# w_down turned by transposing transfers and clipped in two places, the last pair's u by halves, new orders

## The chip, the cores and the metric

The kernel runs on one core of a Trainium2 chip. The metric is the device time of one execution in microseconds: the median of three runs, 260.02 us before the change (259.32 to 260.18). The engines are named as in the profile: PE is TensorE, PEld its weight loads, DVE is VectorE, ACT is ScalarE, POOL is GpSimd, SP is SyncE. A "q" behind a name is the queue from which that engine issues transfers.

## The reference, cut to what matters

```python
def fwht(x): ...             # normalised Walsh-Hadamard transform, last axis
def act_quant(x, bits):      # per token: round(x * 127 / max|x|), clipped, divided again
def weight_quant(w):
    scale = jnp.clip(jnp.mean(jnp.abs(w)), EPS, None)
    q = jnp.clip(jnp.round(w / scale), -1.0, 1.0) * scale
def hbitlinear(x, w, bits):
    xq = act_quant(fwht(x), bits)
    wq = weight_quant(w)
    return jnp.einsum('bsd,fd->bsf', xq, wq)

w = weights[conditions]                        # x: (64, 64, 512), w: (64, 64, 64)
h = jnp.einsum('bct,bcd->bdt', x, w)           # conditional projection
h = hbitlinear(h, w_up, 8)                     # 512 -> 1024
h = jnp.square(jax.nn.relu(h))
x = x + hbitlinear(h, w_down, 8)               # 1024 -> 512
```

## The kernel before

The 64 batches of 64 rows are 16 tiles of 256 tokens; a tile t has two halves k of 128 tokens (a "pair" of batches). For each tile TensorE runs `project(t)` (the conditional product with the first steps of the Hadamard transform, fp32, L870), `had_z(t,k)` (the 128-wide Hadamard step, fp32, L886), `up(t,u)` for u = 0 to 3 (fp16, L911), `had_u(t,k)` (the 128-wide Hadamard step of h, fp32, L934) and `down(t,k)` (fp16, L966). Between them ScalarE copies (`y_split`, L508), quantises z and u to fp16 (`quant_z` L519, `quant_u` L566), applies relu (L526) and square (L533), and issues the transposing transfers of the quantised tiles (`turn_z` L541, `turn_u` L559). VectorE runs the other Hadamard steps (`y_outer` L1207, `g_outer` L1240, `g_inner` L1245), the maxima (`z_absmax` L1224, `u_absmax` L1252) with a small `floor` and `invert` behind each, and the `residual` (L1270), which adds x and writes the output tile. GpSimd runs the last addition and subtraction of a half's Hadamard transform (`g_last`, L373, two instructions) and small factors (`token_units` L358, `u_unscale` L379). SyncE issues the loads of x (L201), the gathers of the conditional weights (L208) and the stores (L222).

Every engine's order is written out by hand as a list of calls, and every call waits on semaphores. u_ps holds one half of u only, so each `had_u` waits until `quant_u` has read the half before it; the second halves of the last two tiles have a home of their own in h_ps. A load of x(t) waits for the residuals of tile t - 8.

The weights: w_up and w_down each come as four pieces of 128 x 1024 fp32. Their absolute values are summed, one scale comes of that, and ScalarE multiplies each piece by the inverse scale into fp16 units of 2^-24 (`weight_round`, L493), where the conversion rounds. `weight_turn` (L854) turns a piece in eight 128x128 transposes on TensorE into u_ps, and `weight_evac` (L1201) copies it out on VectorE with both clips to w_upT or w_downT. `weight_turn(n, u)` for u of 2 or 3 waits for the evacuation two before it. `had_u(0,0)` waits for the evacuations of w_down, as they share u_ps; `down(0,0)` waits for w_downT.

The end: `had_u(15,1)`, `down(13,1)`, `had_u(15,0)`, `down(14,1)`, `down(14,0)`, then both quantised halves of the last tile are turned on TensorE (`last_turn`, L942) and copied by VectorE (`last_copy`, L1219), and `down(15,0)` and `down(15,1)` follow, each with its residual and store.

Of the kernel before, what the change touches and what calls it, by code (L numbers as in the profile page):

```python
# [13 lines left out]
P = 128  # L14
B, C, T = 64, 64, 512
F = 1024
KP = 2
# [27 lines left out]
def ffn_kernel(nc, x, cond, w_cond, w_up, w_down, had, out):  # L45
# [7 lines left out]
    with ctx:  # L53
# [20 lines left out]
        w_downT = sb("w_downT", [P, FC, T], FP16)  # L74
# [18 lines left out]
        u_max = sb("u_max", [P, TILES, KP], FP32)  # L93
        u_abs = sb("u_abs", [P, TILES, KP], FP32)
# [23 lines left out]

        s_cond = sem("cond_loaded")
# [15 lines left out]
        s_wT = [sems(f"wT_ready{n}", 4) for n in range(2)]  # L135
        s_turn = sem("turn_may_start")
# [31 lines left out]
        s_table = sem("table_loaded")  # L168
        s_o = sems("o_ready", KP)
# [27 lines left out]
        def _(sp):  # L197
# [20 lines left out]

            def store(t, k):
# [25 lines left out]
            gather(3, 0)  # L245
            gather(3, 1)
            load_x(3)
# [7 lines left out]
            gather(5, 1)  # L255
            load_x(4)
            load_x(5)
            gather(5, 2)
# [9 lines left out]
            gather(8, 0)  # L268
            gather(8, 1)
            gather(8, 2)  # L270
            load_x(6)
            gather(8, 3)
            load_x(7)
            gather(9, 0)
            gather(9, 1)
            gather(9, 2)
            store(0, 1)
            load_x(8)
            gather(9, 3)
# [3 lines left out]
            store(0, 0)  # L283
# [3 lines left out]
            store(1, 1)  # L287
            store(1, 0)
            load_x(9)
            store(2, 1)  # L290
            gather(11, 2)
            gather(11, 3)
            load_x(10)
            gather(12, 0)
            store(2, 0)
            load_x(11)
            gather(12, 1)
            gather(12, 2)
            gather(12, 3)
            store(3, 1)  # L300
            gather(13, 0)
            gather(13, 1)
            gather(13, 2)
            gather(13, 3)
            gather(14, 0)
            gather(14, 1)
            store(3, 0)
            store(4, 1)
            store(4, 0)
            gather(14, 2)  # L310
            load_x(12)
            gather(14, 3)
            store(5, 0)
            gather(15, 0)
            store(5, 1)
            load_x(13)
            gather(15, 1)
            load_x(14)
            gather(15, 2)
            store(6, 1)  # L320
            store(6, 0)
            load_x(15)
            store(7, 1)
            gather(15, 3)
            store(8, 1)
            store(7, 0)
            store(8, 0)
            store(9, 0)
            store(9, 1)
            store(10, 1)  # L330
            store(10, 0)
            store(11, 1)
            store(11, 0)
            store(12, 0)
            store(12, 1)
            store(13, 1)
            store(13, 0)
            store(14, 0)
            store(15, 0)
            store(14, 1)  # L340
            store(15, 1)
            for i in range(NO):
                for k in range(KP):
                    sp.wait_ge(s_store[i][k], 16 * (TILES // NO))

        @block.gpsimd
        def _(pool):
# [4 lines left out]
                                    base=0, pattern=[[-1, P]], channel_multiplier=1).then_inc(s_ident, 1)  # L352

# [1287 lines left out]
```

## Time and profile before

| | |
|---|---|
| median of three runs | 260.02 us (259.32 to 260.18) |
| the profiled execution | 260.16 us |
| its span, first to last instruction | 258.4 us |
| TensorE busy | 250.6 us, 97% |
| VectorE busy | 206.6 us, 80% |
| ScalarE busy | 146.9 us, 57% |
| GpSimd busy | 107.9 us, 42% |
| DMA, mean | 133 GB/s |

An engine's busy time counts the instructions that work on data; issuing a transfer and waiting don't count. The ends of matmuls are modelled, so the time from the start of a group of matmuls to the start of the next tells more than its busy time. In a timeline a row is a run of equal instructions: start, length, engine, line, operation, output and input, count, and in brackets how long the engine stood idle before it and what released it.

### The profile page before, as it was taken

How to read it: one execution, taken by the hardware profiler on the slowest of the kernel's cores; microseconds unless marked ns; L12 is line 12 of the kernel's file. 1: busy time of each engine (PE TensorE's matmuls, PEld its weight loads, DVE VectorE, ACT ScalarE, POOL GpSimd, SP SyncE). 2: the span in 40 equal slices, each digit the busy share in tenths (PEclk: the TensorE clock that was granted, in tenths of full speed). 3: DMA queues.
4: the chain of work that ended last, by engine and by line, in shares of the span. 5: the costliest groups of instructions: out<-in, count | busy, mean ns of one | idle time of the engine just before them, and what ended most of it. 6: DMA issues, size and time to landing. Idle time of an engine off the chain costs nothing. (4 is left out here: it accounts for less than half of the span.)

```text
span 258.4 us, 6363 instructions
## 1 busy us (share of the span) xinstructions
PE 250.6 (97%) x2218; PEld 208.8 (81%) x2218; DVE 206.6 (80%) x344; ACT 146.9 (57%) x210; POOL 107.9 (42%) x135
## 2 busy tenths in 40 slices
PE   8999999999999999999999999999999999989994
PEld 8988898989888788778997788878898887757651
DVE  0468599979998597897878987989898898999482
ACT  0279797577445756375657275555775647551330
POOL 1000008580707336260807353472935545686710
PEclk9999999999999999999999999999999999999999
DMA  4995162264383272846634981364446757435523
GB/s 109 356 373 186 40 193 54 55 189 91 65 205 97 43 209 57 173 107 156 105 89 124 205 210 26 74 195 83 127 80 86 201 115 133 124 92 109 126 109 137
DMA packets 63442, 34.31 MB, mean 133 GB/s; under 512 B 53554, under 2 KB 53682, under 8 KB 63410
## 3 DMA queue, kind: packets, MB, share of 16 engines
q10 hardware_dynamic: 48370, 12.95, 27.4%
q1 hardware_dynamic: 15040, 20.95, 25.2%
q8 instruction: 18, 0.29, 0.5%
q14 instruction: 14, 0.11, 0.1%
HBM read 13.70 MB, written 8.39 MB: 85 GB/s over the span
## 5 line engine op out<-in xcount | busy, mean ns | idle before, releaser
L373 POOL TENSOR_TENSOR p<-g 128x512 f32<-128x512 f32 x64 | 80.8, 1286 | 126.8 <-DVE g L1245 126.8
L911 PE MATMUL h_ps<-zqT,w_upT 128*128 128x256 f16 x512 | 63.5, 273 | 0.0
L934 PE MATMUL u_ps<-had_sb,p 128*128 128x128 f32 x480 | 59.0, 276 | 1.8 <-ACT uq L566 1.8
L934 PEld LDWEIGHTS u_ps<-had_sb,p 128*128 128x128 f32 x480 | 56.6, 192 | 4.7 <-ACT uq L566 3.2
L966 PE MATMUL o_ps<-w_downT,uqT 128*128 128x512 f16 x240 | 56.7, 379 | 0.2 <-DVE uqT L1219 0.2
L911 PEld LDWEIGHTS h_ps<-zqT,w_upT 128*128 128x128 f16 x512 | 49.4, 98 | 7.8
L566 ACT ACTIVATE uq<-u_ps,u_mul 128x1024 f16<-128x1024 f32 x30 | 33.4, 1112 | 33.9 <-DVE u_mul L1263 27.9
L526 ACT ACTIVATE g<-h_ps 128x512 f32<-128x512 f32 x64 | 37.3, 594 | 25.9 <-PE h_ps L911 18.9
L1252 DVE TENSOR_REDUCE u_max<-u_ps 128x1 f32<-128x1024 f32 x30 | 36.6, 1220 | 11.9 <-PE u_ps L934 11.6
L966 PEld LDWEIGHTS o_ps<-w_downT,uqT 128*128 128x128 f16 x240 | 23.4, 98 | 22.3 <-issue 0.4
L1240 DVE TENSOR_TENSOR g<-g 128x1024 f32<-128x1024 f32 x32 | 40.4, 1288 | 1.0 <-issue 0.7
L1245 DVE TENSOR_TENSOR g<-g 128x1024 f32<-128x1024 f32 x32 | 38.2, 1216 | 0.2
L533 ACT ACTIVATE g<-g 128x1024 f32<-128x1024 f32 x32 | 33.3, 1054 | 3.9 <-issue 2.8
L886 PE MATMUL z_ps<-had_sb,y 128*128 128x128 f32 x248 | 33.6, 278 | 0.3 <-ACT zq L519 0.2
L870 PE MATMUL y_ps<-ws,xs 64*128 64x128 f32 x512 | 32.9, 278 | 0.1
L870 PEld LDWEIGHTS y_ps<-ws,xs 64*128 64x128 f32 x512 | 29.9, 188 | 3.1 <-issue 2.1
L886 PEld LDWEIGHTS z_ps<-had_sb,y 128*128 128x128 f32 x248 | 30.5, 192 | 2.1 <-ACT zq L519 0.7
L519 ACT ACTIVATE zq<-z_ps,z_col 128x512 f16<-128x512 f32 x31 | 21.2, 683 | 17.2 <-DVE z_col L1234 16.1
L1270 DVE SCALAR_TENSOR_TENSOR out_sb<-o_ps,u_deq,xs 128x512 f32<-128x512 f32 x30 | 22.4, 747 | 9.3 <-PE o_ps L966 9.0
L1224 DVE TENSOR_REDUCE z_max<-z_ps 128x1 f32<-128x512 f32 x31 | 21.2, 685 | 6.9 <-PE z_ps L886 6.8
L1207 DVE TENSOR_TENSOR y<-y_ps,y_odd 128x512 f32<-128x512 f32 x32 | 21.1, 684 | 2.6 <-ACT y_odd L508 2.6
L379 POOL TENSOR_SCALAR u_deq<-kappa,down_scale,u_abs 128x1 f32<-128x1 f32 x32 | 17.7, 564 | 5.3 <-DVE u_abs L1258 5.2
(54 smaller groups left out, 136.5 us busy)
## 6 DMA issues: line engine op xcount, KB each, us to landing
xs<-in_x_dram SPq DMA_DIRECT2D x16, 512.0 KB, 4.2
out_dram<-out_sb SPq DMA_DIRECT2D x32, 256.0 KB, 2.4
w_raw<-in_L_ffn_w_down_dram SPq DMA_DIRECT2D x4, 512.0 KB, 6.7
w_raw<-in_L_ffn_w_up_dram ACTq DMA_DIRECT2D x2, 512.0 KB, 5.9
w_raw<-in_L_ffn_w_up_dram SPq DMA_DIRECT2D x2, 512.0 KB, 6.7
ws<-in_L_cond_weights_dram SPq DMA_DIRECT2D x62, 16.0 KB, 2.4
uqT<-uq ACTq DMA_TRANSPOSE x30, 3.2
zqT<-zq ACTq DMA_TRANSPOSE x15, 3.3
```

Of the source, the lines that this page charges most:

```text
L373: nc.gpsimd.tensor_tensor(new[:, :, m, :], old[:, :, 0, :], old[:, :, 1, :], (ALU.add, ALU.subtract)[m]).then_inc(s_p8[k], 1)
L526: nc.scalar.activation(g[t % 2][:, 2 * u:2 * u + 2, :], h_ps[:, u % 2, :, :], ACT.Relu, scale=1.0 / UNIT).then_inc(s_r[u], 1)
L533: nc.scalar.activation(part, part, ACT.Square).then_inc(s_g[v], 1)
L566: nc.scalar.activation(uq[t % 2][:, k, :], u_home(t, k), ACT.Copy, scale=u_mul[:, t, k:k + 1])\
L870: mm = nc.tensor.matmul(y_ps[:, b, l, :, j, :], xs[t % NX][rows, j, h * 256 + l * P:h * 256 + (l + 1) * P], w, start=(h == 0), stop=(h == 1))
L886: mm = nc.tensor.matmul(z_home(t, k)[:, c * P:(c + 1) * P], y[t % 2][:, c % 2, c // 2, k, :, :].rearrange("p b d -> p (b d)"), had_sb[:, : ...
L911: mm = nc.tensor.matmul(h_ps[:, u % 2, i, :].rearrange("p (k n) -> p k n", k=KP), w_upT[:, q, f * P:(f + 1) * P], zqT[t % NZT][:, :, q, :] ...
L934: mm = nc.tensor.matmul(home[:, c * P:(c + 1) * P], p8[t % 2][:, c, k * P:(k + 1) * P], had_sb[:, :], start=True, stop=True)
L966: mm = nc.tensor.matmul(o_home(t, k), uqT[t % 2][:, k, m, :], w_downT[:, m, :], start=(m == 0), stop=(m == FC - 1))
L1240: nc.vector.tensor_tensor(g2[:, n, :, :], g[t % 2][:, 0:4, :], g[t % 2][:, 4:8, :], (ALU.add, ALU.subtract)[n]).then_inc(s_g2, 1)
L1245: nc.vector.tensor_tensor(p4[t % 2][:, :, n, :], g2[:, :, 0:2, :].rearrange("p h a n -> p h (a n)"), g2[:, :, 2:4, :].rearrange("p h a n - ...
L1252: nc.vector.tensor_reduce(u_max[:, t, k:k + 1], u_home(t, k), AX.X, ALU.max, apply_absolute_value=True).then_inc(s_umax[k], 1)
```

## The change

w_down: `weight_round(1, u)` goes from ScalarE to GpSimd, with the clip from above in the same instruction. A new `weight_clip(u)` on VectorE clips from below, in place in SBUF. A new `turn_w(u)` on ScalarE issues a transposing transfer of the piece into w_downT, which is laid out anew ([P, 4, FC, P] instead of [P, FC, T]). The four `weight_turn(1, u)` on TensorE, the four `weight_evac(1, u)` on VectorE and the waits of `had_u(0,0)` go.

The last half, (15,1): `had_u` is cut into two halves of 512 columns, each with its own absmax; one quantisation goes to ScalarE and one to VectorE, the two turned halves go to two homes and are copied by VectorE and ScalarE, and `down` is cut into two halves of 256 output columns, each with its residual and its own store, one issued by SyncE and one by ScalarE.

The orders of all five engines are laid anew. The core:

```diff
-        w_downT = sb("w_downT", [P, FC, T], FP16)
+        w_downT = sb("w_downT", [P, 4, FC, P], FP16)
...
+        HF, HT = F // 2, T // 2
+        uT_half = [uT_ps[1][:, 0:HF], u_ps[:, 0:HT].bitcast(FP16)]
+        o_half = [z_ps[:, 0:HT], u_ps[:, T:T + HT]]
...
+            def weight_round(n, u):
+                pool.wait_ge(s_winv[n], 1)
+                nc.gpsimd.tensor_scalar(w_int[n][u], w_raw[n][:, u * WQ:(u + 1) * WQ], w_inv[:, n:n + 1], UNIT,
+                                        ALU.mult, ALU.min).then_inc(s_wrint[n][u], 1)
...
+            weight_round(1, 0)
+            weight_round(1, 1)
+            weight_round(1, 2)
             g_last(0, 0)
+            weight_round(1, 3)
             token_units(0)
...
+            def turn_w(u):
+                act.wait_ge(s_wclip[u], 1)
+                act.sem_inc(s_turn, 1)
+                act.dma_start(w_downT[:, u, :, :], w_int[1][u], transpose=True).then_inc(s_wT[1][u], 16)
...
+            def quant_half():
+                u_turned(act, TILES - 3, 1)
+                act.wait_ge(s_umul[1], TILES)
+                nc.scalar.activation(uq[(TILES - 1) % 2][:, 1, 0:HF], h_flat[:, 0:HF], ACT.Copy,
+                                     scale=u_mul[:, TILES - 1, 1:2]).then_inc(s_uqhalf[0], 1)
...
             quant_z(2, 0)
+            turn_w(0)
             y_split(3)
+            turn_w(1)
+            relu(1, 0)
             relu(1, 1)
...
+            turn_w(2)
             square(1, 0)
             quant_z(2, 1)
...
             quant_z(3, 0)
+            turn_w(3)
             quant_u(0, 0)
...
+            quant_half()
             quant_u(15, 0)
-            quant_u(15, 1)
+            copy_half_too(1)
+            store_half_too(1)
...
-                if t == 0 and k == 0:
-                    pe.wait_ge(s_wT[1][2], 1)
-                    pe.wait_ge(s_wT[1][3], 1)
...
+            def down_half(c):
+                if c == 0:
+                    pe.wait_ge(s_out[1], TILES - 1)
+                for h in range(2):
+                    pe.wait_ge(s_uqThalf[h], 1)
+                for m in range(FC):
+                    mm = nc.tensor.matmul(o_half[c].rearrange("p (u n) -> p u n", u=2), uqT[(TILES - 1) % 2][:, 1, m, :],
+                                          w_downT[:, 2 * c:2 * c + 2, m, :],
+                                          start=(m == 0), stop=(m == FC - 1))
+                mm.then_inc(s_ohalf[c], 1)
...
             down(13, 0)
-            had_u(15, 1)
+            had_half(0)
+            had_half(1)
             down(13, 1)
             had_u(15, 0)
             down(14, 1)
+            turn_half(0)
             down(14, 0)
+            turn_half(1)
             last_turn(0)
-            last_turn(1)
+            down_half(0)
             down(15, 0)
-            down(15, 1)
+            down_half(1)
...
+            def weight_clip(u):
+                dve.wait_ge(s_wrint[1][u], 1)
+                nc.vector.tensor_scalar(w_int[1][u], w_int[1][u], -UNIT, None, ALU.max)\
+                    .then_inc(s_wclip[u], 1)
```

TensorE's order of the head, before and after (from `had_z(1,1)` to `had_u(0,0)`):

```
before: had_z(1,1) project(2) up(0,2) up(0,3) weight_turn(1,0) had_z(2,0) project(3) up(1,0) up(1,1) had_z(2,1)
        weight_turn(1,2) up(1,3) weight_turn(1,1) project(4) weight_turn(1,3) up(1,2) had_z(3,0) had_u(0,0)
after:  had_z(1,1) project(2) up(0,3) up(0,2) had_z(2,0) project(3) had_z(2,1) up(1,0) up(1,1) up(1,2) up(1,3)
        project(4) had_z(3,0) had_u(0,0)
```

VectorE's order in the same stretch:

```
before: y_outer(2,0) y_outer(2,1) z_absmax(2,0) weight_evac(1,0) ... g_outer(0,0) g_outer(0,1) y_outer(3,0)
        y_outer(3,1) g_inner(0,0) g_inner(0,1) weight_evac(1,1) z_absmax(2,1) ...
after:  y_outer(2,1) y_outer(2,0) weight_clip(1) weight_clip(0) z_absmax(2,0) ... g_outer(0,0) g_outer(0,1)
        weight_clip(2) g_inner(0,1) g_inner(0,0) y_outer(3,1) y_outer(3,0) z_absmax(2,1) ...
```

TensorE's order ahead of the end:

```
before: had_u(12,1) down(10,1) up(15,0) up(15,1) down(11,0) had_u(13,0) up(15,2) up(15,3) down(11,1) had_u(13,1)
        down(12,0) had_u(14,1) down(12,1) had_u(14,0) down(13,0) had_u(15,1) ...
after:  down(10,1) up(14,3) up(14,2) had_u(12,1) down(11,0) up(15,0) up(15,1) had_u(13,0) up(15,3) up(15,2)
        down(11,1) down(12,0) had_u(13,1) had_u(14,1) down(12,1) had_u(14,0) down(13,0) had_half(0) had_half(1) ...
```

VectorE's order between `u_absmax(12,1)` and `g_inner(15,1)` is nearly the same in both; after: `g_outer(14)`, `g_inner(14)`, `u_absmax(13,0)`, `residual(11,1)`, `g_outer(15)`, `g_inner(15,0)`, `u_absmax(13,1)`, `residual(12,0)`, `u_absmax(14,1)`, `g_inner(15,1)`.

## Rows read from the trace of the kernel before

**Rows 1.** The page, part 1: busy us, share of the span, instructions.

```profile
PE 250.6 (97%) x2218; PEld 208.8 (81%) x2218; DVE 206.6 (80%) x344; ACT 146.9 (57%) x210; POOL 107.9 (42%) x135
```

**Rows 2.** Stretches: us, busy us of each engine, TensorE's clock, DMA share, GB/s.

```profile
27.00:44.00 17.00, 16.78 (x206) 15.26 (x203) 14.30 (x26) 13.63 (x21) 4.00 (x7) 1.00 0.34 96
...
55.00:215.00 160.00, 159.39 (x1412) 133.47 (x1410) 137.45 (x230) 96.36 (x140) 73.37 (x95) 1.00 0.56 126
215.00:240.00 25.00, 23.81 (x170) 17.70 (x168) 22.47 (x29) 11.65 (x14) 18.14 (x14) 1.00 0.48 114
```

**Rows 3.** TensorE's waits: waited for, us in total, times, longest.

```profile
PE u_ps L934 <- ACT uq L566: 1.8, 2, 1.2
```

**Rows 4.** Timeline of TensorE in the head.

```profile
36.62 0.61 PE L854 MATMUL u_ps<-ident,w_raw 128*128 128x128 f16 x8
37.06 1.04 PE L911 MATMUL h_ps<-zqT,w_upT 128*128 128x256 f16 x8
...
38.48 2.06 PE L870 MATMUL y_ps<-ws,xs 64*128 64x128 f32 x32
...
43.18 1.95 PE L934 MATMUL u_ps<-had_sb,p 128*128 128x128 f32 x16
```

**Rows 5.** Groups by line: shapes, count, busy us, mean ns, idle before.

```profile
L493 ACT ACTIVATE w_raw<-w_raw,w_inv 128x1024 f16<-128x1024 f32 x8 | 8.9, 1144 | 0.0
L1229 DVE TENSOR_SCALAR z_col<-z_max 128x1 f32<-128x1 f32 x32 | 4.8, 150 | 0.6
L1201 DVE TENSOR_SCALAR w_downT<-u_ps 128x1024 f16<-128x1024 f16 x4 | 2.6, 679 | 0.0
```

**Rows 6.** Timeline of ScalarE and of its queue (ACTq).

```profile
42.22 1.27 ACTq L541 DMA_TRANSPOSE zqT<-zq  x1
43.54 0.60 ACT L526 ACTIVATE g<-h_ps 128x512 f32<-128x512 f32 x1 [0.93 <-issue]
```

**Rows 7.** Timeline of VectorE in the head.

```profile
25.82 0.16 DVE L1181 RECIPROCAL w_inv<-w_scale 128x1 f32<-128x1 f32 x1
...
32.09 0.69 DVE L1224 TENSOR_REDUCE z_max<-z_ps 128x1 f32<-128x512 f32 x1 [1.31 <-PE z_ps L886]
33.94 2.36 DVE L1240 TENSOR_TENSOR g<-g 128x1024 f32<-128x1024 f32 x2 [0.30 <-ACT g L533]
36.22 1.28 DVE L1207 TENSOR_TENSOR y<-y_ps,y_odd 128x512 f32<-128x512 f32 x2
37.41 2.35 DVE L1245 TENSOR_TENSOR g<-g 128x1024 f32<-128x1024 f32 x2
```

**Rows 8.** Timeline of GpSimd in the head.

```profile
39.85 2.50 POOL L373 TENSOR_TENSOR p<-g 128x512 f32<-128x512 f32 x2 [38.23 <-DVE g L1245]
46.90 2.45 POOL L379 TENSOR_SCALAR u_deq<-kappa,down_scale,u_abs 128x1 f32<-128x1 f32 x1 [1.24 <-DVE u_abs L1258]
```

**Rows 9.** Timeline of TensorE near 110 us; then landings of x, 150 to 185 us.

```profile
110.17 1.05 PE L934 MATMUL u_ps<-had_sb,p 128*128 128x128 f32 x7 [0.61 <-ACT uq L566]
...
DMA to landing us min/median/max: 4.2/4.3/4.8
```

**Rows 10.** Timeline ahead of the end; then two pieces of the chain that ended last.

```profile
216.38 1.95 PE L934 MATMUL u_ps<-had_sb,p 128*128 128x128 f32 x16
...
236.72 1.22 DVE L1245 TENSOR_TENSOR g<-g 128x1024 f32<-128x1024 f32 x1
...
240.73 2.02 PE L934 MATMUL h_ps<-had_sb,p 128*128 128x128 f32 x16
...
237.27 1.78 PE u_ps L934 x16
239.06 1.73 PE o_ps L966 x8
```

**Rows 11.** Timeline of the end.

```profile
255.09 0.75 DVE L1270 SCALAR_TENSOR_TENSOR out_sb<-z_ps,u_deq,xs 128x512 f32<-128x512 f32 x1 [0.98 <-PE z_ps L966]
```

**Rows 12.** The page, part 6: issues, KB each, median us to landing.

```profile
out_dram<-out_sb SPq DMA_DIRECT2D x32, 256.0 KB, 2.4
```

More of the change, by code:

```diff
@@ L680, in _ @@
+            quant_z(8, 0)
+            turn_z(7)
             relu(6, 0)
-            quant_z(8, 0)
-            relu(6, 1)
-            turn_u(3, 1)
+            quant_u(4, 0)
             y_split(9)
-            relu(6, 2)
-            turn_z(7)
-            quant_u(4, 0)
+            negate_w(10)
+            quant_z(8, 1)
             relu(6, 3)
             square(6, 0)
+            quant_u(4, 1)
+            turn_z(8)
+            relu(6, 2)
             square(6, 1)
+            relu(7, 1)
@@ L721, in _ @@
+            quant_z(10, 0)
+            negate_w(12)
+            y_split(11)
+            turn_u(5, 1)
+            quant_u(6, 1)
+            square(8, 0)
+            quant_z(10, 1)
+            negate_w(13)
+            relu(8, 3)
             square(8, 1)
-            quant_u(6, 1)
+            turn_z(10)
+            relu(9, 1)
             relu(9, 0)
+            y_split(12)
+            quant_u(7, 0)
+            relu(9, 3)
+            quant_z(11, 0)
             turn_u(6, 1)
-            quant_z(10, 1)
@@ L1058, in _ @@
             down(3, 0)
+            project(9)
             had_u(4, 1)
+            up(6, 2)
             down(3, 1)
             up(7, 1)
+            had_u(5, 0)
             had_z(9, 0)
             up(7, 0)
-            had_u(5, 0)
             project(10)
             up(7, 2)
-            down(4, 0)
             up(7, 3)
@@ L1461, in _ @@
             y_outer(11, 0)
-            g_outer(8, 0)
             y_outer(11, 1)
+            z_absmax(10, 1)
+            z_floor(10, 1)
+            z_invert(10, 1)
             residual(5, 0)
             u_absmax(7, 0)
+            g_outer(8, 1)
+            g_outer(8, 0)
             u_floor(7, 0)
+            residual(5, 1)
+            z_absmax(11, 0)
+            g_inner(8, 1)
+            z_floor(11, 0)
             u_invert(7, 0)
-            z_absmax(11, 0)
-            g_outer(8, 1)
@@ L1470, in _ @@
[L1470 to L1472 removed]
             g_inner(8, 0)
+            y_outer(12, 0)
+            z_invert(11, 0)
+            residual(6, 0)
+            y_outer(12, 1)
             u_absmax(7, 1)
[L1475 to L1476 removed]
             u_floor(7, 1)
             u_invert(7, 1)
[L1479 removed]
             z_absmax(11, 1)
             z_floor(11, 1)
+            g_outer(9, 0)
             z_invert(11, 1)
+            g_outer(9, 1)
@@ L1528, in _ @@
             z_invert(13, 1)
+            g_outer(11, 1)
+            g_inner(11, 1)
             g_inner(11, 0)
-            g_inner(11, 1)
+            residual(8, 0)
             z_absmax(14, 0)
@@ L1539, in _ @@
             residual(8, 1)
+            g_outer(12, 0)
+            g_outer(12, 1)
             z_absmax(14, 1)
-            g_outer(12, 1)
             z_floor(14, 1)
-            g_outer(12, 0)
+            y_outer(15, 0)
             z_invert(14, 1)
-            g_inner(12, 1)
             u_absmax(11, 0)
```

763 lines of the change are left out of this document (400 added, 363 removed).

## The prediction

> **What bounds the kernel now.** I read the page's busy shares first: TensorE is busy for 250.6 us of 258.4, VectorE for 206.6 [rows 1]. Modelled ends can hide waiting, so I then read the table of stretches [rows 2]: TensorE is idle for 0.6 us of the 160 us from 55 to 215 us; VectorE is at 84% from 27 to 44 us and at 90% from 215 to 240 us. Third, TensorE's list of waits: in the middle and at the end it has two for ScalarE's quantisation of u, 1.8 us together [rows 3]. Last, starts of neighbouring TensorE groups: a group that starts later than the work before it takes was kept waiting, also where the row shows no idle time. So TensorE's work sets the pace, with VectorE close behind at both ends, and the clock is full throughout [rows 2].
>
> The profiled execution is 260.16 us, of which the span is 258.4 and 1.76 lies around it. The median of the three runs, 260.02, is 0.14 below. I sum against 260.16 and take off 0.14 at the end.
>
> **Weights, TensorE.** Four turns of w_down go. One took 0.44 us from its start to that of the next group [rows 4], so 1.76 us of TensorE's work goes. The fp32 columns of `down` now come in four runs of 128; `up` already reads its moving tile in two runs and needs 1.04 us with its drain for eight matmuls of 256 columns [rows 4], where `down` needs 1.73 for eight of 512 in one run [rows 10]: no loss by runs, so I price them at nothing.
>
> **Weights, ScalarE.** Four roundings of 1.14 us go [rows 5]. Four transposing transfers come. Issuing one takes ScalarE's queue 1.27 us, during which nothing else starts: an evacuation behind one waited 0.93 us with "issue" as the reason [rows 6]. 4 x 1.14 = 4.6 us out, 4 x 0.93 to 1.27 = 3.7 to 5.1 us in: nothing gained. Queued behind `turn_w(0)` to `turn_w(2)` are `relu(1,0)` to `relu(1,1)` and `quant_z(2,1)`, which TensorE wants; behind `turn_w(3)` stands `quant_u(0,0)`. The Trainium skill (DMA: Bandwidth & Descriptors, "Issuing engines are not separate DMA queues") calls the sequencer's time to start a DMA usually small relative to the DMA. The row shows 1.27 us, more than a rounding. By the rule the head could not lose; its end of -0.3 below stands by the row.
>
> **Weights, GpSimd.** It does nothing until 39.85 us [rows 8], and w_inv is there at 26.0 us [rows 7]. A 128x1024 rounding with one input isn't in the trace. GpSimd's addition takes 1.25 us for 512 outputs from two operands [rows 8]: by outputs the rounding of 1024 takes 2.5 us, by elements read 1.25, and less isn't excluded, as the additions come from a busier stretch, so 0.9 to 2.5 us. I take 1.4: one operand is read. Three end at 30.2 us, and the fourth runs behind `g_last(0,0)`. Up to 3.0 us each this costs nothing (last rival).
>
> **Weights, VectorE.** Four evacuations of 0.68 us become four clips. A 128x1 tensor_scalar takes 0.15 us and an evacuation 0.68 [rows 5]; between these I take 0.4, as the data are 16-bit and no longer in PSUM. That saves 1.1 us (0 to 2.1). Clips 1 and 0 fall into VectorE's idle 1.31 us before 32.09 us [rows 7].
>
> **What is late next in the head.** `project(4)` needs both halves of `y_outer(3)`. Before, VectorE ran g_outer(0) for 2.36 us, then y_outer(3) for 1.28, then g_inner(0) for 2.35 [rows 7]. Now the clip and g_inner stand ahead of y_outer(3). From g_outer's start at 33.3 us (a rounding less on ScalarE, 0.6 earlier): 33.3 + 2.36 + 0.4 + 2.35 + 1.28 = 39.7 us, against a start of `project(4)` at 38.48 [rows 4]. But before, a turn and an `up` still followed; now `project(4)` 1.98, had_z(3,0) 0.9, and had_u(0,0) starts at 39.7 + 2.9 = 42.6, against 43.18 [rows 4]. So of 1.76 us only 0.6 arrives: VectorE's order has become the wait. If g_inner comes earlier than I think, all of it does, with the waits of this stretch 2.3; if the four issues come badly, -0.3.
>
> **Middle (55 to 215 us).** Orders are new; work is equal. One wait of 0.6 us goes: had_u(6,1) waited for ScalarE's quantisation of the half before it [rows 9], and its distance from had_u(6,0) grows from 3.5 us of TensorE work to 4.6. Against that, seven neighbouring `had_u` are now 3.5 us apart where five were, and absmax, floor, inversion and quantisation fill about 3.2 of it. SP's order: `project(13)` now comes 7.3 us of TensorE work behind `down(5,1)`, which frees its x buffer, before 12.5; residual 0.75, stores and issue about 0.9, landing 4.2 to 4.8 [rows 9] make 6.5, so it should hold. I charge 0.4 for new waits: a net gain of 0.2 (from 0.6 to -1.5).
>
> **Tail.** had_u(13,1) is moved two blocks behind had_u(13,0), which takes its 1.2 us wait [rows 3] away. But had_u(15,1) hangs on another chain: g_inner(15,1) on VectorE at 236.72, then GpSimd's two additions, 2.50 [rows 8], then TensorE at 240.73 [rows 10]: 236.72 + 1.22 + 2.50 is 240.4, and the rest are hand-overs. One more `down` now stands ahead of had_u(12,1), so without other gains that ends at 216.38 + 1.73 + 1.95 = 220.1 us; up to the end of what stands ahead of g_inner(15,1) VectorE then has seven g additions of 1.18 [rows 7], four absmax of 1.2 (twice the columns of a z one of 0.69 [rows 7]), three residuals of 0.7 [rows 11] and three pairs of small steps of 0.4 (two of 0.15 with a hand-over), 16.4 us and no gap: 236.5. It takes 0.1 to 0.2; I count 0.1.
> From there to the end of the last residual it was 255.84 - 240.73 = 15.1 us [rows 10, 11]. Now TensorE has two half had_u 1.78, had_u(15,0) 1.78, three `down` and down(15,0) 4 x 1.73, transposes 0.88, two half `down` 1.74: 13.1 us [rows 4, 10]. Ahead of down_half(0), ScalarE's copy of half the tile (0.6, as its evacuation of 512 columns [rows 6]) with two hand-overs of 0.1 and last_turn's 0.44 beside it leaves 0.4 of waiting. Drain and hand-over 0.2, half a residual 0.45 (0.15 to 0.75): 14.2. Gain 0.9 (0.3 to 1.3). The last store is half as large. 256 KB land in 2.4 us [rows 12], 512 KB of x in about 4.3 [rows 9]; on a straight line half a store saves 0.9, if size counts for nothing here, 0. store(15,0), issued some 0.7 earlier at full size, allows little more than 0.7. I take 0.3, nearer to nothing, as other transfers have ended by then.
>
> **Sum:** 0.6 + 0.2 + 0.1 + 0.9 + 0.3 = 2.1; 260.16 - 2.1 - 0.14 = 257.9 us.
>
> **Rivals.** *All TensorE time comes back* (15%): VectorE has slack at both ends after all; 1.76 + 0.6 + 1.2 + 0.9 + 0.5 = 5.0, so 255.0. For it: TensorE's 0.6 us of idle in the middle; against: VectorE's 84 and 90% [rows 2].
> *VectorE and ScalarE set the pace* (18%): the head returns nothing, three of the tight had_u pairs wait 0.5 us each against the 0.6 that goes, and only the tail's 1.3 stays: 260.02 + 1.5 - 0.6 - 1.3 = 259.6, within 0.3%; with two more such waits 260.6. For it: the same shares; against: the pairs' small steps follow one another directly in the new order.
> *The roundings come late* (12%, slower): GpSimd's u_deq, one column, took 2.45 us [rows 8] beside two of VectorE's additions with two SBUF operands, 2.36 in all [rows 7]. If a rounding of 2.5 us is held up by 2.4, it takes 4.9. VectorE stops at clip 0 until two are done, 26.0 + 2 x 4.9 = 35.8 us, where its slack ends at 32.1: 3.7 us that y_outer(3) and so TensorE lose; 257.9 + 3.7 = 261.6. It decides from 3.0 us each. Against: no such addition runs from 26 to 33 us [rows 7]. The Trainium skill (SBUF — State Buffer, "Who interferes with whom") says the same and that a 2-port VectorE operation, as the clip may be, shuts GpSimd out for its length; u_deq's row agrees for two operands, no row here shows the clip.
> That GpSimd rounds otherwise than ScalarE would alter the result, not the time.
>
> **Chances.** Forecast 55%, with its own range 256.4 to 259.2; the rivals as above. The range reaches from the first rival to the second's upper side, 254.8 to 260.7 with 0.1 to 0.2 of rounding, and leaves out the third. A measurement can tell 0.3% (0.8 us) from no change. Faster 0.72: forecast, first rival, a little of the second; same 0.16; slower 0.12.
>
> **What would show it.** Turns of w_raw on TensorE 32 instead of 64; 49 transposing issues on ScalarE; GpSimd's rounding near 1.4 us; VectorE's clip near 0.4. `project(4)` waiting for y_outer(3), had_u(0,0) near 42.6; had_half(0) within 1.5 us of 239.8; last residual about 14.2 us behind it. I'm wrong if had_u(0,0) starts before 41.5 or after 43.5, if roundings take over 3 us, or if new waits between 55 and 215 us pass 1.5 us.

## The result and the profile after

The changed kernel takes 261.34 us (median of six, 260.83 to 261.85) beside 260.10 us of the kernel before on the same chip: a ratio of 1.0055 (1.0039 to 1.0070). It is slower by 1.2 us where I forecast 2.1 faster, and its time lies outside my range. Its executions are of two kinds, which can't be understood without the clock: three at 260.83 to 260.97 us with a mean granted clock of 1.000, and three at 261.70 to 261.85 with 0.993, among them the profiled one, of 261.85 us with a span of 260.0.

Busy shares first (page, part 1), beside [rows 1]:

```profile
PE 250.2 (96%) x2194; PEld 208.4 (80%) x2194; DVE 206.6 (79%) x348; ACT 145.3 (56%) x207; POOL 120.1 (46%) x139
```

TensorE is as busy as before although four turns are gone, and only GpSimd has grown, by 12.2 us. Next, TensorE's waits (waited for, us in total, times, longest):

```profile
PE z_ps L944 <- ACT zq L554: 2.6, 2, 2.3
PE o_ps L1051 <- DVE out_sb L1392: 1.2, 2, 1.0
```

The two waits of [rows 3] are gone, and two new ones are there. The longer one is in the head, where the four timelines are read from TensorE backwards. TensorE:

```profile
32.25 2.06 PE L928 MATMUL y_ps<-ws,xs 64*128 64x128 f32 x32
36.64 2.07 PE L944 MATMUL z_ps<-had_sb,y 128*128 128x128 f32 x8 [2.34 <-ACT zq L554]
38.51 4.41 PE L969 MATMUL h_ps<-zqT,w_upT 128*128 128x256 f16 x32
...
45.83 1.95 PE L989 MATMUL u_ps<-had_sb,p 128*128 128x128 f32 x16
```

ScalarE and its queue:

```profile
35.90 0.69 ACT L554 ACTIVATE zq<-z_ps,z_col 128x512 f16<-128x512 f32 x1 [2.67 <-DVE z_col L1319]
36.36 1.27 ACTq L573 DMA_TRANSPOSE w_downT<-w_raw  x1
37.74 0.60 ACT L543 ACTIVATE y_odd<-y_ps 128x512 f32<-128x512 f32 x1 [1.15 <-issue]
```

VectorE:

```profile
33.15 1.67 DVE L1285 TENSOR_SCALAR w_raw<-w_raw 128x1024 f16<-128x1024 f16 x2 [2.11 <-POOL w_raw L382]
34.74 0.68 DVE L1309 TENSOR_REDUCE z_max<-z_ps 128x1 f32<-128x512 f32 x1
...
38.00 0.42 DVE L1285 TENSOR_SCALAR w_raw<-w_raw 128x1024 f16<-128x1024 f16 x1
...
47.54 1.36 DVE L1285 TENSOR_SCALAR w_raw<-w_raw 128x1024 f16<-128x1024 f16 x1
```

GpSimd:

```profile
25.73 11.06 POOL L382 TENSOR_SCALAR w_raw<-w_raw,w_inv 128x1024 f16<-128x1024 f32 x3 [24.10 <-DVE w_inv L1266]
40.77 2.50 POOL L404 TENSOR_TENSOR p<-g 128x512 f32<-128x512 f32 x2 [3.98 <-DVE g L1330]
43.25 3.70 POOL L382 TENSOR_SCALAR w_raw<-w_raw,w_inv 128x1024 f16<-128x1024 f32 x1
```

A rounding takes 3.70 us, not 1.4. The second ends at 33.1, and VectorE, whose order has the clips 1 and 0 ahead of z_absmax(2,0), stands still for 2.11 us. z_absmax(2,0) starts at 34.74, though had_z(2,0), whose result it reads, had started at 31.19 and run for 1.13 us, up to 32.32. Of these 2.4 us some 0.8 are the rounding's and 1.6 the two clips': the first of them, which starts 0.1 us behind the start of the third rounding, takes 1.33 us, the second 0.41 (the row above gives 1.67 for both). Floor and inversion come late, then quant_z(2,0), for which ScalarE stands idle 2.67 us, and TensorE waits 2.34 us ahead of had_z(2,1). After that TensorE's granted clock falls (stretches: us, busy us of TensorE, clock, DMA share, GB/s):

```profile
35.00:37.00 2.00, 0.36 (x1) 0.91 1.05 406
37.00:39.00 2.00, 2.00 (x11) 0.50 0.76 166
39.00:41.00 2.00, 2.00 (x15) 0.74 1.18 109
41.00:43.00 2.00, 2.00 (x20) 1.00 0.47 103
```

0.50 is the 1.2 GHz level of its two. had_u(0,0) starts at 45.83 instead of 43.18 [rows 4]: 2.65 us lost. The tail:

```profile
232.18 1.90 PE L1051 MATMUL o_ps<-w_downT,uqT 128*128 128x512 f16 x8 [1.02 <-DVE out_sb L1392]
...
243.15 2.02 PE L997 MATMUL h_ps<-had_sb,p 128*128 128x128 f32 x16
...
257.16 0.48 DVE L1368 SCALAR_TENSOR_TENSOR out_sb<-u_ps,u_deq,xs 128x256 f32<-128x256 f32 x1
```

The block that hangs on g_last(15,1) starts at 243.15, before at 240.73 [rows 10]: 2.42 us late, so the head's loss has gone through the middle nearly whole. From there to the last residual's end it is 14.49 us where it was 15.11, and from that to the end of the span 2.36 for 2.56. The difference of the two profiled executions adds up: +2.65 in the head, -0.23 up to had_half(0), -0.62 in the last stretch, -0.20 in the store, +0.09 around the span, +1.69 us in all.

### The profile page after: what moved, and what is told of

The parts are those of the page before. It is cut to its first block, busy times and chain, and to the rows that moved or that the text cites. A ratio compares the mean times of both kernels' runs of the same rounds, so it can differ in the third digit from the quotient of the medians.

```text
span 260.0 us, 6332 instructions
## 1 busy us (share of the span) xinstructions
PE 250.2 (96%) x2194; PEld 208.4 (80%) x2194; DVE 206.6 (79%) x348; ACT 145.3 (56%) x207; POOL 120.1 (46%) x139
## 4 chain that ended last, share of the span: by engine, by line
PE 77%; DVE 7%; ACT 4%; DMA 3%; issue 3%; POOL 3%; ACTq 1%; DVEq 0%
PE h_ps L969 19%; PE u_ps L989 19%; PE o_ps L1051 19%; PE z_ps L944 9%; PE y_ps L928 8%; DMA w_raw<-in_L_ffn_w_up_dram 3%; POOL w_raw L382 3%; ACT w_raw L528 2%; DVE g L1325 1%; DVE g L1330 1%; DVE w_raw L1285 1%; ACT w_junk L523 1%; ACT zq L554 1%; DVE out_sb L1392 1%; PE h_ps L997 1%
## 5 line engine op out<-in xcount | busy, mean ns | idle before, releaser
L624 ACT ACTIVATE uq<-u_ps,u_mul 128x1024 f16<-128x1024 f32 x30 | 33.4, 1113 | 25.8 <-DVE u_mul L1385 25.8
L1325 DVE TENSOR_TENSOR g<-g 128x1024 f32<-128x1024 f32 x32 | 38.7, 1230 | 1.4 <-ACT g L568 1.3
L1330 DVE TENSOR_TENSOR g<-g 128x1024 f32<-128x1024 f32 x32 | 38.2, 1218 | 0.2
L944 PE MATMUL z_ps<-had_sb,y 128*128 128x128 f32 x248 | 34.4, 283 | 3.0 <-ACT zq L554 2.6
L944 PEld LDWEIGHTS z_ps<-had_sb,y 128*128 128x128 f32 x248 | 31.5, 196 | 5.1 <-ACT zq L554 3.0
L382 POOL TENSOR_SCALAR w_raw<-w_raw,w_inv 128x1024 f16<-128x1024 f32 x4 | 14.8, 3702 | 24.1 <-DVE w_inv L1266 24.1
```

The lines of the kernel that those rows point to most:

```text
L624: nc.scalar.activation(uq[t % 2][:, k, :], u_home(t, k), ACT.Copy, scale=u_mul[:, t, k:k + 1])\
L944: mm = nc.tensor.matmul(z_home(t, k)[:, c * P:(c + 1) * P], y[t % 2][:, c % 2, c // 2, k, :, :].rearrange("p b d -> p (b d)"), had_sb[:, : ...
L1325: nc.vector.tensor_tensor(g2[:, n, :, :], g[t % 2][:, 0:4, :], g[t % 2][:, 4:8, :], (ALU.add, ALU.subtract)[n]).then_inc(s_g2, 1)
L1330: nc.vector.tensor_tensor(p4[t % 2][:, :, n, :], g2[:, :, 0:2, :].rearrange("p h a n -> p h (a n)"), g2[:, :, 2:4, :].rearrange("p h a n - ...
```

## The experiments

Three theories at first: the length of the rounding sets the head (A); the new orders hold it anyway (B, later O for orders); GpSimd and VectorE contend for SBUF (C). The fall of the clock is a fourth term, to be measured apart. Every ratio is to the kernel before, run beside it on the same chip.

**A quarter of each rounding.** It leaves out three quarters of w_down, which count as zero.

```diff
-  tensor_scalar(w_int[n][u],                w_raw[n][:, u*WQ:(u+1)*WQ],      ...)
+  tensor_scalar(w_int[n][u][:, 0:WQ // 4],  w_raw[n][:, u*WQ:u*WQ + WQ//4],  ...)   # w_int in a zeroed tile
```

> The changed kernel with all its orders, but GpSimd rounds only the first 256 of the 1024 columns of each piece of w_down; the other columns of the rounded piece are zeros (a tile of its own, cleared ahead), so three quarters of w_down count as zero. Only the length of the rounding changes. Theory A (the roundings of 3.70 us hold VectorE at its clips, TensorE then waits 2.34 us and its clock falls): roundings near 1.1 us, the clips start by 31.5 us, no wait of more than 0.6 us ahead of had_z(2,1), had_u(0,0) starts near 42.6 instead of 45.83, the clock stays full, time 257.5 to 259. Theory B (the new orders and ScalarE's four transposing issues hold the head whatever GpSimd does): had_u(0,0) still after 44.5, time above 260.

259.42 us, ratio 0.9995 (0.997 to 1.002): even with the kernel before, no more. GpSimd, then ScalarE and its queue, then TensorE:

```profile
25.88 3.38 POOL L388 TENSOR_SCALAR w_zero<-w_raw,w_inv 128x256 f16<-128x256 f32 x3 [20.79 <-DVE w_inv L1272]
...
29.05 0.31 ACT L543 ACTIVATE ws<-ws 128x128 f32<-128x128 f32 x1 [1.28 <-DMA ws<-in_L_cond_weights_dram]
...
36.28 1.93 ACTq L579 DMA_TRANSPOSE w_downT<-w_zero  x1
38.26 0.60 ACT L567 ACTIVATE g<-h_ps 128x512 f32<-128x512 f32 x1 [1.48 <-issue]
...
32.00 1.13 PE L950 MATMUL z_ps<-had_sb,y 128*128 128x128 f32 x8 [1.22 <-DVE y L1298]
...
38.91 1.92 PE L975 MATMUL h_ps<-zqT,w_upT 128*128 128x256 f16 x16 [0.93 <-ACT g L567]
...
43.74 1.95 PE L995 MATMUL u_ps<-had_sb,p 128*128 128x128 f32 x16
```

With a rounding of 1.13 us, below the one I had assumed, the wait of had_z(2,1) is gone, and yet had_u(0,0) starts at 43.74 and not at 42.6. Two other waits are left: negate_w(3), moved ahead of y_split(2), waits for its gather, and relu(1,0) stands behind the issue of turn_w(1). The first depends on when the gather lands: ScalarE waited 1.28 us for it here and not at all at that place in the changed kernel's profile. So with the orders as they are the length of the rounding is worth about 1.6 us (ratio 1.0055 against 0.9995), and the other 1.1 are held by these two waits and by what stands behind them.

**The clips later.** VectorE takes clips 1, 2 and 3, and ScalarE turn_w(1) to turn_w(3), some places further back; the roundings are whole.

```diff
-  weight_clip(1) weight_clip(0) z_absmax(2,0)        z_absmax(3,0) weight_clip(3)
+  weight_clip(0) z_absmax(2,0) ... weight_clip(1) g_inner(0,1) weight_clip(2) g_inner(0,0) ... u_invert(0,0) weight_clip(3)
```

> The changed kernel with full roundings on GpSimd; only VectorE's four clips and ScalarE's four transposing issues are moved later in their queues: clip 0 where clips 1 and 0 stood, clip 1 ahead of g_inner(0,1), clip 2 behind it, clip 3 behind u_invert(0,0); turn_w(1) behind relu(1,1), turn_w(2) behind relu(1,3), turn_w(3) behind relu(2,1). Theory A: roundings stay 3.7 us, VectorE no longer stops for them, had_z(2,1) waits under 0.6 us, had_u(0,0) starts at 42.5 to 43.5, clock full, time 258 to 259.3. Theory B: as before the move, had_u(0,0) after 44.5 and time above 260. If the roundings' contention with VectorE is the cost (theory C), the g additions beside them take clearly more than 1.2 us each.

261.56 us (260.79 to 263.66), ratio 1.0085 (1.0054 to 1.0117). GpSimd rounds from 25.96 to 37.12 us. VectorE, then TensorE:

```profile
34.53 2.36 DVE L1325 TENSOR_TENSOR g<-g 128x1024 f32<-128x1024 f32 x2
...
41.30 2.06 PE L928 MATMUL y_ps<-ws,xs 64*128 64x128 f32 x32 [1.20 <-issue]
...
57.16 1.89 PE L1051 MATMUL o_ps<-w_downT,uqT 128*128 128x512 f16 x8 [1.50 <-DMA w_downT<-w_raw]
```

The wait of had_z(2,1) is gone here too, with full roundings, but project(4) now waits 1.20 us for y_outer(3) behind g_inner, and down(0,0) 1.50 us for the last part of w_down; had_z(2,0) waits 1.48, as the gather landed late here too. had_u(0,0) starts at 44.28, earlier than the 45.83 of the changed kernel's profile, between what the two theories had forecast, and down(0,0) loses that again: a late clip pays later. The two additions of g_outer(0) run beside the third rounding from start to end and take 2.36 us, as before the change without one [rows 7]. So a rounding doesn't lengthen these additions. It does lengthen a clip: the 1.33 us of clip 1 in the changed kernel are theory C's, in another place.

**TensorE kept busy through the wait**, with nine matmuls whose result nobody reads.

```diff
   project(3)
+  idle(9, ...)
   had_z(2,1)
```

> The changed kernel with nine matmuls on a tile of ones put between project(3) and had_z(2,1), about 2.2 us of TensorE work that nobody reads, in the stretch in which TensorE waits 2.34 us. Theory A with the clock as a part of the cost: the granted clock stays 1.00 in every run, the runs are no longer of two kinds (260.9 and 261.8), all lie near 260.9 or 0.2 above; had_z(2,1) starts as late as before. If the clock has nothing to do with the two kinds of runs, both stay.

260.92 us (260.61 to 261.61), ratio 1.0051 (1.0029 to 1.0073); all six executions show a mean clock of 0.999 or 1.000. TensorE (each of the nine appears as two), then the stretch:

```profile
35.09 2.27 PE L895 MATMUL o_ps<-ones 128*128 128x128 f32 x18
...
45.03 1.95 PE L989 MATMUL u_ps<-had_sb,p 128*128 128x128 f32 x16
```

```profile
37.00:39.00 2.00, 2.00 (x21) 1.00 1.12 138
```

The clock no longer falls, and the time is that of the changed kernel's executions at full clock. So the fall costs 0.9 us, the distance of its two kinds, in half of its executions, and the wait as such the larger rest. That the matmuls kept the clock is likely but not shown by this run alone: in its profile negate_w(3) waited 1.31 us for its gather, so project(3) came later and only some 1.6 us were left to fill, less than a wait of 1.76 us that left the clock alone in another kernel (below). They also ran on for 0.5 us past the end of quant_z(2,0).

**Four forms of the rounding**, one for each quarter of w_down: multiplication and clip to 16 bits, multiplication alone, both to 32 bits into a spare tile, and a constant multiplier. The third and fourth quarters are not scaled and rounded as they should be.

```diff
+  u == 0: mult w_inv, min UNIT -> fp16     u == 1: mult w_inv -> fp16
+  u == 2: mult w_inv, min UNIT -> fp32     u == 3: mult 1.0, min UNIT -> fp16
```

> The changed kernel; the four roundings on GpSimd are four forms of the 128x1024 tensor_scalar, each into a tile beside w_raw: piece 0 as it is (per-partition multiplier, then a minimum, fp16 out), piece 1 with the multiplication alone, piece 2 with fp32 out, piece 3 with a constant multiplier. Pieces 1 to 3 of w_down are therefore not what they should be. If the price comes from the second operation, piece 1 takes about half of 3.7 us; if it comes from the fp16 output, piece 2 does; if from the per-partition operand, piece 3 does; if from contention with VectorE (theory C), the lengths follow what VectorE runs beside them and not the form.

```profile
25.68 3.70 POOL L391 TENSOR_SCALAR w_zero<-w_raw,w_inv 128x1024 f16<-128x1024 f32 x1 [20.61 <-DVE w_inv L1281]
29.36 2.85 POOL L393 TENSOR_SCALAR w_zero<-w_raw,w_inv 128x1024 f16<-128x1024 f32 x1
32.18 3.70 POOL L395 TENSOR_SCALAR w_wide<-w_raw,w_inv 128x1024 f32<-128x1024 f32 x1
...
42.32 3.63 POOL L397 TENSOR_SCALAR w_zero<-w_raw 128x1024 f16<-128x1024 f32 x1
```

One execution, 259.81 us. Neither the type of the result nor the multiplier by partition makes the length; the second operation does, by 0.85 us.

**The old tail.** The changed kernel with the last pair of u in one piece, as before.

```diff
-  had_half(0) had_half(1) down(13,1) had_u(15,0) down(14,1) turn_half(0) down(14,0) turn_half(1) last_turn(0) down_half(0) down(15,0) down_half(1)
+  had_u(15,1) down(13,1) had_u(15,0) down(14,1) down(14,0) last_turn(0) last_turn(1) down(15,0) down(15,1)
```

> The changed kernel with the last pair of u in one piece again, as before: had_u(15,1), last_turn(1), last_copy(1), down(15,1), one store. Head and middle stay. If the halves are worth what the changed kernel's trace shows between the start of had_u(15,0) and the last residual (14.49 us where before showed 15.11) and in the store (0.2 us), this kernel is 0.8 us slower than the changed one, 262.0 to 262.2 us. If the shorter last stretch only takes up a wait that the rest leaves anyway, it is within 0.3 us of the changed kernel.

262.6 us (262.39 to 263.41), ratio 1.0100 (1.0069 to 1.0131). All four executions are at a mean clock of 0.991 to 0.993; the changed kernel's at that clock are at 261.70 to 261.85. TensorE, then VectorE:

```profile
243.02 2.02 PE L985 MATMUL h_ps<-had_sb,p 128*128 128x128 f32 x16
...
257.39 0.75 DVE L1385 SCALAR_TENSOR_TENSOR out_sb<-z_ps,u_deq,xs 128x512 f32<-128x512 f32 x1 [0.98 <-PE z_ps L1047]
```

From 243.02 to 258.14 it is 15.12 us, as in the kernel before; 2.56 us follow up to the span's end of 260.7. The halves are worth 0.8 us.

**Short roundings and two moves** on ScalarE, in the kernel with a quarter of each rounding.

```diff
-  negate_w(3) quant_z(1,1) y_split(2)         turn_w(1) relu(1,0) relu(1,1) turn_w(2)
+  quant_z(1,1) y_split(2) negate_w(3)         relu(1,0) relu(1,1) turn_w(1) turn_w(2)
```

> The kernel with a quarter of each rounding (it rounds 256 of 1024 columns, the rest of w_down counts as zero), with two moves in ScalarE's order: negate_w(3) behind y_split(2), and relu(1,0), relu(1,1) ahead of turn_w(1). Theory O (orders): with the roundings short, what is left of the head's missing gain is those two places, so the waits of had_z(2,0) (1.2 us) and of the third part of up(1) (0.9 us) go, had_u(0,0) starts at 41.6 to 42.6 us instead of 43.74, and the kernel takes 257.6 to 258.4 us. Theory S (something else is as late): one of the two waits comes back at the next instruction, had_u(0,0) stays after 43.2, and the time stays within 0.4 us of 259.4.

259.18 us (258.09 to 260.02), ratio 0.9957 (0.9936 to 0.9978). Both waits go, and the next ones are there, as theory S has it:

```profile
39.60 2.06 PE L934 MATMUL y_ps<-ws,xs 64*128 64x128 f32 x32 [0.70 <-issue]
42.45 1.16 PE L950 MATMUL z_ps<-had_sb,y 128*128 128x128 f32 x8 [0.80 <-ACT zq L560]
43.45 1.95 PE L995 MATMUL u_ps<-had_sb,p 128*128 128x128 f32 x16
```

project(4) waits for y_outer(3), which VectorE runs behind the clips and g_inner. That is the order that I had named in the prediction, with 39.7 us for this start, and it holds the head with short roundings too. The second wait isn't VectorE's: its inversion for had_z(3,0) starts at 40.32 us and takes 0.16, but ScalarE starts quant_z(2,1) only at 41.73, as square(1,0) ahead of it waited 2.98 us behind the issues of turn_w(1) and turn_w(2).

**The head's orders anew**, once with the rounding as it is, once with the multiplication alone on GpSimd, both clips in VectorE's one instruction and the fourth rounding ahead of g_last(0,0).

```diff
   VectorE: weight_clip(0) z_absmax(2,0) z_floor z_invert weight_clip(1) g_outer(0,0) g_outer(0,1)
+           y_outer(3,1) y_outer(3,0) [weight_clip(2)] g_inner(0,0) z_absmax(2,1) z_floor z_invert g_inner(0,1)
            # second kernel: weight_clip(2) ahead of y_outer(3,1), weight_clip(3) ahead of g_inner(0,1)
   ScalarE: quant_z(1,1) y_split(2) negate_w(3) ... quant_z(2,0) y_split(3) turn_w(0) negate_w(4) relu(1,0) relu(1,1) turn_w(1) ...
   TensorE: project(3) up(1,0) had_z(2,1) up(1,1)
```

> The changed kernel's computation in full, with the head's orders laid otherwise: negate_w(3) behind y_split(2); clip 1 behind z_invert(2,0), clip 2 behind y_outer(3); y_outer(3), g_inner(0,0) and z_absmax(2,1) in that order; the relus ahead of turn_w(1), turn_w(2) behind relu(1,2); up(1,0) ahead of had_z(2,1). GpSimd's roundings stay at 3.70 us. Theory A (the length of the rounding sets the head): clip 1 still waits for the second rounding, which ends at 33.1, and g_last(0,0) stays behind the third, so had_u(0,0) starts after 43.2 and the kernel takes 259.6 us or more. Theory O (the orders set it): had_u(0,0) starts at 41.2 to 42.8 and the kernel takes 257.6 to 258.8 us.

> As the kernel with the orders laid otherwise, and GpSimd's rounding with the multiplication alone (2.85 us in the look at the forms) and both clips in VectorE's one instruction; the fourth rounding comes ahead of g_last(0,0), ending near 37.1 us. All of w_down is computed. Theory A: four roundings take 11.4 us instead of 14.8, and the head gains on the kernel with the same orders by up to 0.9 us, had_u(0,0) at 40.9 to 42.3, the time 257.0 to 258.3 us. Theory O: with the orders mended the rounding's length has no more influence, both kernels are within 0.3 us. A clip of both sides takes 0.42 us alone, as the one-sided does.

262.05 us (ratio 1.0066, 1.0040 to 1.0093) and 261.69 us (1.0050, 1.0017 to 1.0083). The first lies within theory A's bounds, but not by A's cause, as GpSimd had been idle for 4.83 us when g_last(0,0) began; the second fits neither theory. I had made a mistake of my own, which GpSimd's row of the second kernel shows:

```profile
41.83 2.49 POOL L404 TENSOR_TENSOR p<-g 128x512 f32<-128x512 f32 x2 [3.41 <-DVE g L1330]
```

g_last(0,0) waits for both g_inner, and I had set z_absmax(2,1) between them. had_u(0,0) started at 44.33 and 44.37 us, behind waits of 1.76 and 2.09. In the first of the two kernels all four executions kept the clock at 1.00; in the second, four of five had a mean of 0.992 or 0.993, and the fifth, at full clock, took 260.20 us. So at full clock the second is ahead by 1.9 us, by this one execution: in the first VectorE stopped for another 2.96 us at clip 3, waiting for the fourth rounding, and had_z(3,1) waited 1.14.

**That mistake mended**, with the multiplication alone (clip 3, turn_w(2) and turn_w(3) move too):

```diff
   y_outer(3,1) y_outer(3,0)
+  g_inner(0,1) g_inner(0,0) z_absmax(2,1) z_floor(2,1) z_invert(2,1) weight_clip(2) y_outer(4,0)
```

> As the kernel with the multiplication alone on GpSimd and both clips on VectorE, with VectorE's order mended: g_last(0,0) waits for both g_inner(0,0) and g_inner(0,1), so both stand directly behind y_outer(3), ahead of z_absmax(2,1) and of clip 2; turn_w(2) goes out behind turn_z(2). g_inner then ends near 39.2 us, g_last(0,0) near 41.7. Theory V (VectorE's serial chain from w_down's clips to g_inner(0,1) sets the head): had_u(0,0) starts at 41.7 to 42.7 us instead of 44.37, TensorE has no wait over 1 us in the head, its clock stays at 1.00, and the kernel takes 258.2 to 259.2 us, below the kernel before. Theory W (the head cannot be had without the work that stood in TensorE's queue before): another wait of over 1 us appears ahead of had_u(0,0) or of down(0,0), and the time stays at 260 us or more.

**258.36 us** (258.11 to 258.55), ratio 0.9945 (0.9927 to 0.9963): faster than both kernels. GpSimd, then TensorE:

```profile
25.62 12.82 POOL L382 TENSOR_SCALAR w_raw<-w_raw,w_inv 128x1024 f16<-128x1024 f32 x4 [24.01 <-DVE w_inv L1266]
39.37 2.69 POOL L404 TENSOR_TENSOR p<-g 128x512 f32<-128x512 f32 x2 [0.92 <-DVE g L1330]
...
42.11 2.05 PE L989 MATMUL u_ps<-had_sb,p 128*128 128x128 f32 x16
```

From 25 to 44 us no wait of TensorE is over 0.5 us, and had_u(0,0) starts 1.07 us earlier than before [rows 4]. The theory of VectorE's chain (V) holds in start, waits, clock and time. The four roundings took 2.84, 2.84, 3.18 and 4.03 us: the last two ran beside VectorE's g additions, which did not grow (2.35 us a pair).

**The same orders with two operations** on GpSimd, which is the only difference from the kernel before it here:

> The kernel with VectorE's order mended, all orders the same, and GpSimd's rounding with its two operations again (multiplication and one clip, 3.70 us in place of 2.85). The roundings end at 29.4, 33.1, 36.8 and 40.5 us, so g_last(0,0) can start only at 40.5 and had_u(0,0) at 43.1 or later. Theory R (the rounding's length still decides): the kernel is 0.8 to 1.6 us slower than the one with the multiplication alone. Theory O (only the orders decide): within 0.4 us of it.

GpSimd, then VectorE's clip 1, then TensorE:

```profile
25.67 14.73 POOL L382 TENSOR_SCALAR w_raw<-w_raw,w_inv 128x1024 f16<-128x1024 f32 x4 [24.05 <-DVE w_inv L1266]
40.37 2.68 POOL L404 TENSOR_TENSOR p<-g 128x512 f32<-128x512 f32 x2
...
33.19 1.23 DVE L1285 TENSOR_SCALAR w_raw<-w_raw 128x1024 f16<-128x1024 f16 x1
...
41.97 1.16 PE L944 MATMUL z_ps<-had_sb,y 128*128 128x128 f32 x8 [1.20 <-ACT zq L554]
43.10 2.05 PE L989 MATMUL u_ps<-had_sb,p 128*128 128x128 f32 x16
```

259.24 us (ratio 0.9974, 0.9962 to 0.9985), 0.88 us more, and had_u(0,0) 0.99 later. Two chains end there together. The four roundings, all 3.70 us again, end 2.0 us later, and g_last(0,0) waits for them; and clip 1, just behind the start of the third rounding, takes 1.23 us where it took 0.41, so that z_absmax(2,1) comes 0.88 later and had_z(3,0) waits 1.20 us. Read the other way: with full roundings of two operations, the orders (and a clip of both sides on VectorE) bring the changed kernel from a ratio of 1.0055 to 0.9974, that is 2.1 us.

**One `up` moved near the end**, to cover the wait of down(12,0), in the fastest kernel.

```diff
-  had_u(13,0) up(15,3) up(15,2) down(11,1) down(12,0)
+  had_u(13,0) up(15,3) down(11,1) up(15,2) down(12,0)
```

> The same kernel with one more move near the end: down(11,1) ahead of up(15,2), so that up(15,2) (0.87 us) stands between down(11,1) and down(12,0), which waits 1.02 us for residual(11,1) in the changed kernel's trace (1.18 us from start to start). If that wait is simply uncovered, it falls to 0.3 us and the kernel is 0.7 to 0.9 us faster than the one without the move. If it is VectorE that is late there, had_half(0) waits longer for g_last(15,1) and the two kernels are within 0.3 us.

262.39 us (260.88 to 262.69), ratio 1.0090 (1.0065 to 1.0115): 2.6 us more with the clock at 1.00, 4.0 in the median, as four of its six executions have a mean clock of 0.993. Both expectations were wrong. ScalarE, VectorE, TensorE:

```profile
227.79 1.08 ACT L561 ACTIVATE g<-h_ps 128x512 f32<-128x512 f32 x2 [2.74 <-PE h_ps L969]
...
230.50 3.33 DVE L1325 TENSOR_TENSOR g<-g 128x1024 f32<-128x1024 f32 x2 [1.88 <-ACT g L568]
...
236.95 1.90 PE L1051 MATMUL o_ps<-w_downT,uqT 128*128 128x512 f16 x8 [2.03 <-DVE out_sb L1392]
```

down(12,0) waits 1.02 us as before: residual(11,1) has its place in VectorE's order and hasn't moved. But the last relu of h comes 1.86 us later, and VectorE, busy with hardly a gap in this stretch of the fastest kernel, then has 1.88 us of idle time that nothing gives back. Its two additions behind that take 3.33 us instead of 2.36, beside two u_unscale of GpSimd that take 3.70. These 1.9 and 1.0 us are the loss: g_inner(15,1) starts 2.7 us later. So TensorE's wait of 1.02 us is slack that VectorE's chain leaves, and work put into it is missing where VectorE waits for that work.

## Why the prediction was wrong

**"Weights, GpSimd" failed first.** I took 1.4 us for a rounding, with 0.9 to 2.5 as bounds, from rows of an addition [rows 8]. It takes 3.70 in all four. The addition of two operands, 1.25 us for 512 outputs, is no upper bound for a tensor_scalar of two operations: at the same count of outputs the latter is half as long again. I had written that up to 3.0 us it costs nothing; past that the stop of VectorE and the wait of TensorE behind it came as described. Short roundings alone give back 1.6 us, the fall of the clock included; other orders alone, with roundings of 3.70, give back 2.1; one operation and the orders together 2.9. So what costs is the two together, a long rounding and a clip that collects it too early, and the shares don't add up. Of the signs that I had named for being wrong, two came: roundings over 3 us, and had_u(0,0) behind 43.5.

**"Weights, VectorE" failed in its sum.** I took 0.4 us a clip and placed clips 1 and 0 in idle time. Alone a clip does take 0.42, but the four took 1.33, 0.41, 0.42 and 1.36, 3.5 us in all where I had 1.6 and the evacuations had taken 2.7 [rows 5]: not 1.1 us saved but 0.8 lost. The 0.9 us by which clip 1 grew stand in the chain that TensorE waited for.

**"What is late next in the head" had VectorE right and ScalarE too cheap.** Even with 1.13 us a rounding, had_u(0,0) stood at 43.74 us, where my sum had 42.6. The sum followed VectorE's order alone, and that part held: with short roundings and two moves project(4) started at 39.60, where I had 39.7, and without a wait behind it had_u(0,0) would have stood near 42.6. I had named the relus and quant_z(2,1) behind turn_w, and given the issues -0.3 at worst. With short roundings relu(1,0) behind turn_w(1), whose issue took 1.93 us there, kept TensorE waiting 0.93 us, and with the two moves quant_z(2,1) kept it waiting 0.80, for 43.45. The move of negate_w(3) ahead of y_split(2) I had not followed; it costs what its gather is late, 1.22 us for TensorE in that run. In the changed kernel's profile none of the three shows, as the wait for the clips came earlier: project(4), which I had expected to wait for y_outer(3), follows up(1) without a wait.

**The clock had no term in the sum.** I had noted it as full throughout; a wait of 2.34 us, which the change added, was followed by the 1.2 GHz level in the profiled execution; half of the executions show the lower mean clock, and they take 0.9 us longer. At full clock the changed kernel is at 260.9, still slower than before.

**The third rival had the mechanism**, VectorE's stop at the clips, and at 261.6 us nearly the time, with 12%; the nearness of the time is luck. Its formula for VectorE's stop, 26.0 + 2r, gives 33.4 with r = 3.70, and the clips start at 33.15. Its cause was wrong: I let contention stretch a rounding of 2.5 us to 4.9, where it is 3.70 by itself, with no such addition beside it. Such contention exists, but it struck elsewhere: clip 1 grew from 0.42 to 1.33, and a rounding of one operation from 2.84 to as much as 4.03. Its price was off as well: the stop kept TensorE 2.34 us and not 3.7, and the clock came on top. A chance drawn from the cause, not from the price that decides, came out too small.

**What held.** Issues of turn_w took 1.25 to 1.28 us. `down` still starts 1.73 us apart with four runs of 128. The middle gave 0.28 us from had_u(0,0) to had_u(13,0), against 0.2, the last stretch 0.62 against 0.9, and the store 0.20 against 0.3, all within their bounds; had_half(0)'s chain gave -0.05 where I had 0.1 to 0.2; the old tail's run confirms the last stretch and the store together, 0.8 us. And the kernel with the head mended took 258.36 us with had_u(0,0) at 42.11, near the 257.9 and 42.6 that I had summed, though by another way, with roundings of 2.84 us or more and other orders: what I forecast is about what the idea allows, not what these orders do.

The sum once more, in the profiled execution: the head was to give 0.6 and took 2.65, the rest was to give 1.5 and gave 0.96. The head's miss is 3.25 us, all others 0.54.

## What to carry to other kernels

Price a new kind of instruction on an engine by a row of that kind or let its range reach well past the nearest other kind, and write down the length from which it decides: here I had reckoned with 3.0 us, and the rounding took 3.70. When work goes to an idle engine, look at the instruction that collects it: an engine that runs in order stops everything behind that instruction, so it belongs where the result is surely there, and each move must be followed on every queue that it passes. A wait of the pace-setting engine can be the free end of another engine's chain: before covering it, ask what the cover delays.

## What the runs showed of the hardware

- GpSimd's tensor_scalar of 128x1024 from 32 bits took 3.70 us with two operations, to 16 bits as to 32, 2.85 with one, and 1.13 with two on a quarter of the columns; VectorE adds as many pairs of 32-bit elements in 1.18 [rows 7] and clips as many of 16 bits in 0.42. The Trainium skill (GPSIMD Engine Reference, "Engine selection") calls one-input work on GpSimd roughly line-rate; these rows disagree.
- VectorE's clip took 0.42 us while GpSimd was idle and 0.41 to 0.42 in the middle of a rounding of two operations; it took 1.33 (changed kernel) and 1.23 (mended orders, two operations) when it started just behind a rounding's start, and 1.36 beside GpSimd's additions. The Trainium skill (SBUF — State Buffer, "Who interferes with whom") says that of a VectorE operation of this kind in a 2-port mode and GpSimd, whichever is issued first fully blocks the other for its whole length; the rows agree only in that there is contention, as a clip in the middle of a rounding wasn't held.
- Beside VectorE's additions GpSimd's rounding of two operations stayed at 3.70 us, and that of one operation grew from 2.84 to 3.18 and 4.03; the additions kept their 2.35 us a pair. Beside two u_unscale of one column, near the end, a pair of them took 3.33.
- Waits are known only for the profiled executions. With one of 2.34 us there, TensorE's mean granted clock was 0.993 in three of six executions of the changed kernel (0.50, the 1.2 GHz level, in the stretch behind the wait); with 2.24 it was 0.991 to 0.993 in all four with the old tail, and with 2.09 in four of five with the multiplication alone. It kept its 2.4 GHz level with 1.76 us in all four, and in all six where matmuls filled the wait. With 2.03 us, near the end in the kernel with the moved `up`, it kept it in the profiled execution and one more and was at 0.993 in four. One execution each with a quarter of the roundings and with later clips, whose waits are 1.5 us at most in the profile, had a mean of 0.992 and 0.993 as well: what decides between executions is open; when the gather for negate_w(3) lands, and with it how long the wait is, is one candidate.
- Issuing a transposing transfer of 128x1024 held ScalarE's queue for 1.25 us or more; turn_w(1) took 1.93 us in the kernel with quarter roundings and 2.12 in the fastest one, against 1.25 in the changed kernel.
